# Four float32 matmuls on 32-column quarters in place of three fp32r passes for each 128x128x512 product

## What is computed

```python
x = x + xattn(layernorm(x), ctx_4096, ...)         # top-k masks, sums, conv, gates
# attention: 32 query heads of 64 features, 8 key/value heads, blocks of 64 tokens
q, k, v = h @ wq, h @ wk, h @ wv                   # h = layernorm(x)
...                                                # rope, causal softmax per block
x = x + out @ wo
# feed-forward: one dense layer, biased, plus 8 experts of rank 16, two per token
logits = h @ gate_w.T                              # h = layernorm(x)
...
x = x + h @ base_w.T + base_b + 2.0 * lora_out
```

## Time and profile before

| | us |
|---|---|
| median of 3 runs | 2186.81 |
| lowest and highest run | 2186.34, 2188.13 |
| span of the profiled execution, first to last instruction | 2183.2 |
| matrix part in it, first to last of L1974 to L1976 | 812.2 to 2179.2 |

### The profile page before, as it was taken

How to read it: one execution, slowest core, us unless ns; L and a number is a source line. 1 busy time by engine, 2 the same in 40 slices (tenths; PEclk the granted TensorE clock), 3 DMA queues, 4 the chain that set the end, 5 groups by cost and what they waited for, 6 DMA issues and landing times. The chain is left out here.

```text
span 2183.2 us, 37919 instructions
## 1 busy us (share of the span) xinstructions
PE 1895.6 (87%) x14321; PEld 1532.8 (70%) x14321; DVE 1302.3 (60%) x2085; ACT 1126.1 (52%) x2525; POOL 1076.3 (49%) x927
## 2 busy tenths in 40 slices
PE   4678789777733658999999999999999999999999
PEld 3566667666531257888878888888878888888887
DVE  5999999999999898644435501244445316631111
ACT  7999999999945674333323322232324223322221
POOL 2333344344437406656645556566646445545554
PEclk9999999999976779999999999999999999999999
DMA  9999999999901036422254442222254345334443
GB/s 388 400 394 394 362 356 354 340 346 351 344 32 78 19 87 188 147 86 84 82 178 141 139 140 101 83 88 86 81 197 144 125 161 187 121 129 132 151 145 108
DMA packets 158390, 407.58 MB, mean 187 GB/s; under 512 B 15616, under 2 KB 44544, under 8 KB 156544
## 3 DMA queue, kind: packets, MB, share of 16 engines
q1 hardware_dynamic: 157920, 403.52, 52.4%
q0 software_dynamic: 288, 1.64, 0.2%
HBM read 379.93 MB, written 25.17 MB: 186 GB/s over the span
## 5 line engine op out<-in xcount | busy, mean ns | idle before, releaser
L1417 POOL TENSOR_TENSOR t<-t,t 128x512 fp32r<-128x512 f32 (+1 forms) x488 | 656.0, 1357 | 654.1 <-ACT t L1410 582.6
L1974 PE MATMUL ps<-t,t 128*128 128x512 f32 x1856 | 735.0, 396 | 11.1 <-POOL t L1417 5.7
L1976 PE MATMUL ps<-t,t 128*128 128x512 f32 x1856 | 723.9, 390 | 0.0
L1975 PE MATMUL ps<-t,t 128*128 128x512 f32 x1856 | 723.4, 390 | 0.0
L1410 ACT ACTIVATE t<-t 128x512 fp32r<-128x512 f32 (+1 forms) x488 | 293.6, 609 | 693.0 <-PE ps L1976 383.8
L796 PE MATMUL ps<-t,t 128*128 128x128 bf16 (+1 forms) x5889 | 401.1, 221 | 168.0 <-DVE t L479 156.1
L796 PEld LDWEIGHTS ps<-t,t 128*128 128x128 bf16 x5889 | 342.0, 100 | 246.8 <-DVE t L479 218.5
L479 DVE TENSOR_SCALAR t<-t,t 128x1601 bf16<-128x1601 f32 x453 | 465.8, 1054 | 4.9 <-PE ps L796 0.3
L708 ACT ACTIVATE t<-t,t 128x1601 int8<-128x1601 f32 x256 | 419.1, 1637 | 7.9 <-DVE t L638 7.8
L1974 PEld LDWEIGHTS ps<-t,t 128*128 128x128 f32 x1856 | 348.8, 188 | 89.7 <-POOL t L1417 9.5
L1976 PEld LDWEIGHTS ps<-t,t 128*128 128x128 f32 x1856 | 348.7, 188 | 73.9
(11 more groups left out here) (238 smaller groups left out, 1794.0 us busy)
## 6 DMA issues: line engine op xcount, KB each, us to landing
t<-ctxT SPq DMA_DIRECT2D x256, 800.5 KB, 6.8
t<-wqkv SPq DMA_DIRECT2D x192, 256.0 KB, 3.1
t<-wo SPq DMA_DIRECT2D x128, 256.0 KB, 4.5
t<-wb SPq DMA_DIRECT2D x128, 256.0 KB, 3.4
t<-xT SPq DMA_DIRECT2D x48, 256.0 KB, 7.1
t<-x1d SPq DMA_DIRECT2D x32, 256.0 KB, 4.8
x2d<-t SPq DMA_DIRECT2D x32, 256.0 KB, 2.0
t<-x2d SPq DMA_DIRECT2D x8, 1024.0 KB, 6.3
```

The lines of the kernel that those rows point to most:

```text
L1417: e.tensor_tensor(wlo[r][:, 0:nk, :], raw[r][:, 0:nk, :], wh[r][:, 0:nk, :].bitcast(F32), ALU.subtract).then_inc(w_lo, 1)
L1974: e.matmul(bank[:, :], wh[r][:, q, :], xl, start=(kt == 0), stop=False)
L1975: e.matmul(bank[:, :], wlo[r][:, q, :], xh, start=False, stop=False)
L1976: m = e.matmul(bank[:, :], wh[r][:, q, :], xh, start=False, stop=(c == NCH[p] - 1 and q == nk - 1))
```

## The change

For each product, `mm_tensor` issues four plain float32 matmuls in place of the three fp32r ones: columns 0 to 31 of the raw weights chunk times the operand into partitions 0 to 31 of the bank, then 32 to 63, 64 to 95 and 96 to 127. The operand is the buffer that held the high part; all buffers are now plain float32, so the copy that made the high part is exact, and the low parts, which are still computed, are not read. The weights are no longer split: ACT's and POOL's steps go, and their buffers become raw ones, 12 in place of 4. SP loads chunk n + 10 at chunk n's place, 4 to 10 at chunk 0's, and waits for `group` of the chunk that had the buffer; PE waits for the DMA itself. Six of the 12 DMA semaphores are new, six are those of the ctx ring, counted on from their last value. The gate logits become one float32 matmul of 32 columns for each of the 16 rows of weights.

```diff
+NW, AHEAD = 12, 10
...
-    ATH = at(0, [NT, HT], F32R)
-    ATL = at(32 * KB, [NT, HT], F32R)
+    ATH = at(0, [NT, HT], F32)
+    ATL = at(32 * KB, [NT, HT], F32)
...
-    XL_ = at(64 * KB, [NT, HT], F32R)
-    XH_ = at(96 * KB, [NT, HT], F32R)
+    XL_ = at(64 * KB, [NT, HT], F32)
+    XH_ = at(96 * KB, [NT, HT], F32)
...
-    raw = [sb([4, 128]) for _ in range(4)]
-    wh = [sb([4, 128], F32R) for _ in range(4)]
-    wlo = [sb([4, 128], F32R) for _ in range(4)]
+    raw = [sb([4, 128]) for _ in range(NW)]
...
-        for n in range(3):
-            weights_scalar(e, n)
...
-    d_w = [sem(f"d_w{i}") for i in range(4)]
-    w_hi, w_lo, group = sem("w_hi"), sem("w_lo"), sem("group")
+    d_w = [(sem(f"d_w{i}"), 0) for i in range(6)] + [(d_ring[i], 16 * len(range(i, B * NT, NR))) for i in range(6)]
+    group = sem("group")
...
-        if n >= 4:
-            e.wait_ge(w_lo, n - 3)
-        e.dma_start(raw[n % 4][:, 0:chunk_rows(n), :], weights_of(*CHUNKS[n])).then_inc(d_w[n % 4], 16)
-
-    def weights_scalar(e, n):
...
-        e.activation(wh[r][:, 0:nk, :], raw[r][:, 0:nk, :], ACT.Copy).then_inc(w_hi, 1)
-
-    def weights_gpsimd(e, n):
...
-        e.tensor_tensor(wlo[r][:, 0:nk, :], raw[r][:, 0:nk, :], wh[r][:, 0:nk, :].bitcast(F32), ALU.subtract).then_inc(w_lo, 1)
+        if n >= NW:
+            e.wait_ge(group, n - NW + 1)
+        e.dma_start(raw[n % NW][:, 0:chunk_rows(n), :], weights_of(*CHUNKS[n])).then_inc(d_w[n % NW][0], 16)
+
+    def weights_landed(e, n):
+        signal, base_ = d_w[n % NW]
+        e.wait_ge(signal, base_ + 16 * (n // NW + 1))
...
             for kt in range(4 * c, 4 * c + 4):
-                w = ggf[:, 16 * kt:16 * kt + 128]
-                e.matmul(b1[:, :], w, lo[:, kt, :], start=(kt == 0), stop=False)
-                m = e.matmul(b1[:, :], w, hi[:, kt, :], start=False, stop=(kt == 15))
+                m = e.matmul(b1[0:32, :], ggf[:, 16 * kt:16 * kt + 32], hi[:, kt, :], start=(kt == 0), stop=(kt == 15))
...
             for c in range(NCH[p]):
-                if CH0[p] + c:
-                    weights_sync(e, CH0[p] + c + 3)
+                n = CH0[p] + c
+                for k in range(n + AHEAD if n else 4, n + AHEAD + 1):
+                    weights_sync(e, k)
                 jobs(p, c)
...
-                r, nk = n % 4, chunk_rows(n)
-                e.wait_ge(w_lo, n + 1)
+                w, nk = raw[n % NW], chunk_rows(n)
+                weights_landed(e, n)
...
-                    xh, xl = (XH[:, kt, :], XL[:, kt, :]) if c < 4 else (low[h][0][:, :], low[h][1][:, :])
-                    e.matmul(bank[:, :], wh[r][:, q, :], xl, start=(kt == 0), stop=False)
-                    e.matmul(bank[:, :], wlo[r][:, q, :], xh, start=False, stop=False)
-                    m = e.matmul(bank[:, :], wh[r][:, q, :], xh, start=False, stop=(c == NCH[p] - 1 and q == nk - 1))
+                    xh = XH[:, kt, :] if c < 4 else low[h][0][:, :]
+                    for g in range(0, 128, 32):
+                        m = e.matmul(bank[g:g + 32, :], w[:, q, g:g + 32], xh, start=(kt == 0), stop=(c == NCH[p] - 1 and q == nk - 1))
                 m.then_inc(group, 1)
```

More of the change, by code:

```diff
@@ L5 @@
 F32 = mybir.dt.float32
-F32R = mybir.dt.float32r
 BF16 = mybir.dt.bfloat16
@@ L336, in build @@
     sumsu = sums[:, :].bitcast(U32)
-    lgh = at(stat_off, [HT], F32R)
-    lgl = at(stat_off + 2 * KB, [HT], F32R)
+    lgh = at(stat_off, [HT], F32)
+    lgl = at(stat_off + 2 * KB, [HT], F32)
     t2 = at(qs_off, [HT])
-    ggf = sb([16 * NT + 112], F32R)
+    ggf = sb([16 * NT + 112], F32)
     gg = ggf[:, 0:16 * NT].rearrange("p (t a n) -> p t a n", a=2, n=8)
@@ L357, in build @@
     A2 = stat[:, 1, :, :]
-    low = [(lgh, lgl), (at(mask_off, [HT], F32R), at(mask_off + 2 * KB, [HT], F32R))]
+    low = [(lgh, lgl), (at(mask_off, [HT], F32), at(mask_off + 2 * KB, [HT], F32))]
     ps = [nc.alloc_psum_tensor(f"ps{i}", [128, 512], F32) for i in range(8)]
@@ L1398, in weights_sync @@
             return
-        if n >= 4:
-            e.wait_ge(w_lo, n - 3)
-        e.dma_start(raw[n % 4][:, 0:chunk_rows(n), :], weights_of(*CHUNKS[n])).then_inc(d_w[n % 4], 16)
-    def weights_scalar(e, n):
-        if n >= len(CHUNKS):
-            return
-        r, nk = n % 4, chunk_rows(n)
-        e.wait_ge(d_w[r], 16 * (n // 4 + 1))
-        if n >= 4:
-            e.wait_ge(group, n - 3)
-        e.activation(wh[r][:, 0:nk, :], raw[r][:, 0:nk, :], ACT.Copy).then_inc(w_hi, 1)
-    def weights_gpsimd(e, n):
[L1413 to L1416, removed]
-        e.tensor_tensor(wlo[r][:, 0:nk, :], raw[r][:, 0:nk, :], wh[r][:, 0:nk, :].bitcast(F32), ALU.subtract).then_inc(w_lo, 1)
+        if n >= NW:
[4 more added lines that the diff above has]
+        e.wait_ge(signal, base_ + 16 * (n // NW + 1))
     def operand(p):
@@ L1864, in mm_scalar @@
             for c in range(NCH[p]):
-                weights_scalar(e, CH0[p] + c + 3)
                 jobs(p, c)
@@ L1878, in mm_scalar @@
                 e.activation(low[h][0][:, :], t2[:, :], ACT.Copy).then_inc(low_hi, 1)
[L1880 to L1884, removed]
     def mm_gpsimd(e):
         e.wait_ge(p_lo, 7)
-        weights_gpsimd(e, 2)
         for p, (kind, h, i, nb) in enumerate(PROJ):
-            for c in range(NCH[p]):
-                weights_gpsimd(e, CH0[p] + c + 3)
             if p and PROJ[p - 1][:2] == ("k", 0):
@@ L2015, in _ @@
             stats_gpsimd(e)
-            conv_gpsimd(e)
             mm_gpsimd(e)
```

## The result

The changed kernel takes 2529.39 us (median; 2526.97 to 2530.4) against 2186.81 us: 1.1561 of the time before, 95% interval 1.1539 to 1.1582. That is 342.6 us more; forecast were 374 more, 2561 us, and the range 2475 to 2700 holds it. The profiled span is 2528.6 us against 2183.2.

A forecast was written before the change was run, and what follows sets the result against it. The matrix part was taken as bound by PE's rate of starting matmuls. Products +343, gate logits +13, tile modes +24 and waits -6 made +374 us, giving 2561 us; range 2475 to 2700.

The forecast's parts named there:

- The price after: Matrix products after the change: four quarters run at once, 0.86 us a product, 1596 us against 1253, +343 us.
- Bounds of 0.840 and 0.883: Limits on the new product's time in us: streaming slope alone, and 0.86 plus the 64x64 case's loss per record.
- the loss of the 64x64 tiles: Scores and values in the earlier trace: 64 ns a record against 52 of streaming, 11.5 ns lost per record.
- The price before: Matrix products before the change: three fp32r matmuls at 0.225 us make 0.675 us a product, 1253 us for 1856.
- Gate logits: Gate logit matmuls: 64 fp32r records become 64 float32 records at 0.43 us on one column tile, +13 us.
- Tile modes: PE's trips between tile cuts: 47 new at 0.3 us, +14, and refilling four tiles, +10; together +24 us.
- Waits for POOL: PE's waits for POOL's conversion of weights, 5.7 us in the matrix part, go: taken as -6 us (0 to -10).
- Weights, cover, end: Weights by DMA ten chunks ahead, later x loads, longer last record: nothing taken, up to 5 us for the loads.
- Two at a time: Rival in the products: quarters' pairs overlap only by one record, 1.72 us a product, 4157 us in all; chance 0.09.
- no overlap: Rival in the products: quarters run one after another, 3.44 us a product, about 7350 us in all; chance 0.02.
- the loss that grows: Rival in the products: side-by-side tiles slow by 64/52, 1.06 us a product, about 2930 us; chance 0.05.
- The full rate: Rival in the products: 32-column records stream at full rate, 0.45 us a product, about 1800 us; chance 0.03.

The follow-up runs named there:

- full width: Changed kernel with one plain float32 matmul of 128 columns per product in place of four quarters, gate logits still on 32 columns: 2516.76 us.
- the orders of issue: Changed kernel with two, four, or three then one calls put on a tile before the next quarter: 2531.59, 4290.41 and 3116.14 us.

## Why the prediction was right, step by step

**The price after.** Taken 0.86 us, measured 0.859 by the stretch in the chain and 0.858 from start to start, as with full width. Bounds of 0.840 and 0.883 were wider than needed; the loss of the 64x64 tiles in the earlier trace rows does not appear with 512 columns.

**The price before: the step that was off.** I read 0.675 us from a window of the earlier trace rows that I took for all fp32r but for one pair. It also holds two blocks of four short transposes (L1477, 0.11 us each), which I counted as passes. A window without them:

```profile
1970.00:2170.00 200.00, 200.00 (x884) 165.62 (x883) 33.63 (x36) 49.76 (x87) 104.44 (x87) 1.00 0.42 137
```

884 records touch the window, about 882 fit into it: 0.2267 us a pass, 0.680 a product. The term is +331, not +343; about 10 us of the difference are this price, 3 the 0.86.

**Gate logits.** Forecast 13 us more. Rows of the timeline of the changed kernel, over one chunk:

```profile
1929.38 0.63 PE L1949 MATMUL ps<-t,t 128*32 128x512 f32 x3
1929.81 0.59 PE L1706 MATMUL ps<-t,t 128*32 128x512 f32 x1
1929.84 4.00 PE L1949 MATMUL ps<-t,t 128*32 128x512 f32 x29
1933.67 3.17 PE L1706 MATMUL ps<-t,t 128*32 128x512 f32 x7
1936.25 0.63 PE L1949 MATMUL ps<-t,t 128*32 128x512 f32 x3
```

From 1929.38 to 1936.25 are 6.87 us for four products (3.44) and four logit calls: 3.43 for these, 8 x 3.43 = 27.5 us in all, +13, as taken.

The same rows show the order of starts. The program issues the eight records of the logits (the last stands at 1929.81), then the next chunk. Yet three L1949 records start at 1929.38, 0.43 us before the last logit record. They must be the first ones of the other three quarters, since those of the first quarter stand behind the logits on the same tile. At that moment, in the order of the program, the first tile has the seventh logit record running and behind it the eighth and the two records of the chunk's first quarter: four, the depth that the orders of issue gave. Nothing is gained by the early start, because the first tile, with 16 records of 0.429 us, sets the pace.

**Tile modes.** Forecast 0.3 us for each of 47 new trips, 14 us, and 10 more to refill four tiles. The trips are there: a block of transposes takes 0.59 us in the chain, and the stretch of products behind it 0.14 more than its products (10.44 us for 96 records, where twelve products are 10.30): 0.73 us, 0.72 by the starts around all 36 blocks, against 0.44 to 0.46 for such a block before and 0.44 in the full-width run. The 10 us of refill are not: the blocks of scores and values, which had their trips before, cost 0.62 + 0.47 + 0.14 = 1.23 us where the kernel before lost 1.30 (940.48 - 938.73 less two passes of 0.227). That term was wrong.

**Waits for POOL.** Forecast -6, measured -6 to -7 by the run without the split.

**All terms together.** Both traces, counted block by block (what a block adds to the distance between the starts of the products around it), give: logits and the small matmuls behind them +12.8, 36 blocks of transposes +9.5, the sums over partitions +1.3, blocks with scores or values -3.6, two blocks of transposes and values that hold a wait +0.8, gaps between products -6.6, and -1.5 because products of three passes were a little longer than 0.680 us behind a restart. That is the +12.7; the matrix part is 1710 us long, where I foretold 1740. So of the 31 us by which the forecast was too high, 12 or 13 are the product, 16 are the tile modes (8 measured, 24 taken) and 2 the waits; the errors point the same way and didn't cancel. The later start of the matrix part, 2 us, was in no term, and the median of the runs grew by 3 us less than the profiled span.

**Weights, cover, end.** Nothing taken, nothing found: no wait for DMA with ten chunks or with three. No wait of PE for the x loads that start later shows either.

**Rivals.** Two at a time, no overlap and the loss that grows fall with 0.859 us and with the two quarters left out. The argument against two at a time, that a second record can wait at its tile, is confirmed and sharper: three can. The full rate falls with the 592 ns of a record and the 0.858 us of a product.

On the Trainium skill: its four passes for true FP32 (FP8 and Floating Point Precision, TensorE Precision Notes) agree with this trace as a count of work, if each of the two records stands for two of them: 0.215 us each, so 0.859 and not the 0.90 that I worked out from single passes. That a record is two passes no run shows. Its rule that matmuls start in program order (TensorE: Matmul & The Clock Gate, Part 3, The mechanism) doesn't hold here: it is broken in the rows of the gate logits above, and it doesn't fit the runs with one and with two calls a tile. By it the changed kernel would have taken 1.72 us a product.

## What to carry to other kernels

When a kernel is bound by starts of matmuls, count the records and what each costs from start to start before anything else: three passes of 0.227 us beat one float32 pair of 0.858, and splitting the pair over column tiles saves nothing and costs the trips between tile modes, 0.28 us for each block of other work. Freeing two other engines was worth 0.3%. Whether tiles pay where an operand is too small to fill the array no run here shows. And price a pass in a window that holds nothing else: a dozen short records in it moved this forecast by 10 us.

## What the runs showed of the hardware that I had not expected

- A column tile takes four records, one running and three parked, and what is issued behind them to other tiles starts ahead of them (1929.38 against 1929.81 us). Two and four records in a row to a tile give the same 0.859 us a product; with six a chunk of 3.43 us takes 4.45, with eight 7.02.
- A 512-column pass costs 0.227 us as a single-pass record, fp32r or bf16, but 0.215 in a float32 record of two (0.429). Each change between the two types adds about 0.01 us (0.71 us for a product with two changes, against 0.68). That the longer float32 record is two passes is a reading.
- Two of four quarters left out save nothing (2528.11 us against 2529.39).
- A block of four transposes costs 0.44 us between full-width products and 0.72 between products on 128x32 tiles.
